# Attention over image pairs: keys and values in PSUM banks of their own, values projected behind the context

## The reference

```python
x0 = _gn(x)                                     # group norm, 32 groups
xn = group_norm(x0, gn1_w, gn1_b, 32)
qkv = einsum('oc,bchw->bohw', qkv_w, xn) + qkv_b   # 3 x 128 rows: 8 heads of 16
q, k, v = split(qkv, 3)                         # q * 0.25
q_norm = softmax(q, axis=-1)                    # over the 256 pixels
k_norm = softmax(k, axis=-2)                    # over the 16 channels of a head
context = einsum('bhdn,bhen->bhde', k_norm, v)
out = einsum('bhde,bhdn->bhen', context, q_norm)
out = einsum('oc,bchw->bohw', out_w, out) + out_b
x = x + group_norm(out, gn2_w, gn2_b, 1) + x0
```

## Time and profile before

| | |
|---|---|
| median of 3 runs | 54.88 us (54.81 to 56.35) |
| the profiled execution | 54.68 us |
| its span, first to last instruction | 52.9 us |
| PE busy | 43.9 us (83%), 434 records |
| PE weight loads busy | 29.2 us (55%) |
| VectorE busy | 41.3 us (78%), 141 instructions |
| ScalarE busy | 30.9 us (58%) |
| GpSimd busy | 26.3 us (50%) |
| mean granted TensorE clock | 0.985 |

### The profile page before, as it was taken

One profiled execution on the slowest core, in us unless ns is written; L12 is line 12 of the kernel. 1 busy time (PEld: TensorE's weight loads), 2 busy tenths in 40 slices (PEclk: granted clock), 3 DMA queues, 4 the chain that ended last, 5 costly groups with the idle time before them and its releaser, 6 DMA issues.

```text
span 52.9 us, 1397 instructions
## 1 busy us (share of the span) xinstructions
PE 43.9 (83%) x434; PEld 29.2 (55%) x434; DVE 41.3 (78%) x141; ACT 30.9 (58%) x98; POOL 26.3 (50%) x55
## 2 busy tenths in 40 slices
PE   2999999993999399569989999998998998995200
PEld 2774747851665346454675666666577464843100
DVE  0039999999998999989699969969969998634730
ACT  0723008949902574599768696696485776358400
POOL 5000221938689218724864984685689920041700
PEclk9999999999999999999999999999999999999985
DMA  0597960000000000000030020021002000020222
GB/s 0 148 323 235 364 221 2 0 0 0 0 0 6 0 0 12 0 0 0 0 105 0 12 97 2 0 74 32 0 1 98 12 0 6 0 93 11 95 99 99
DMA packets 2823, 2.84 MB, mean 54 GB/s; under 512 B 256, under 2 KB 2816, under 8 KB 2816
## 3 DMA queue, kind: packets, MB, share of 16 engines
q1 hardware_dynamic: 2528, 2.49, 14.7%
q10 hardware_dynamic: 288, 0.27, 1.4%
HBM read 1.71 MB, written 1.05 MB: 52 GB/s over the span
## 4 chain that ended last, share of the span: by engine, by line
PE 46%; DVE 31%; issue 13%; ACT 4%; POOL 0%; DVEq 0%; ACTq 0%; POOLq 0%
PE kv_ps L450 8%; PE kv_ps L414 7%; PE o_ps L528 5%; PE o_ps L505 4%; PE q_ps L469 4%; PE kv_ps L438 4%; PE o_ps L491 4%; DVE nqmax L716 3%; PE q_ps L466 3%; DVE kmx L699 3%; DVE ctxm L758 3%; DVE res L800 2%; DVE xstat L599 2%; PE o_ps L516 2%; DVE vs L739 2%
## 5 line engine op out<-in xcount | busy, mean ns | idle before, releaser
L348 ACT ACTIVATE eq<-q_ps,nqmax 128x256 f32<-128x256 f32 x16 | 7.4, 474 | 3.2 <-DVE nqmax L716 3.2
L265 POOL TENSOR_TENSOR orstd<-ve,minus_half 128x1 f32<-128x1 f32 x8 | 4.4, 552 | 9.1 <-DVE ve L782 9.1
L450 PE MATMUL kv_ps<-w_all,xn 64*128 64x256 f32 x64 | 8.3, 379 | 0.0
L414 PE MATMUL kv_ps<-ones 128*128 128x512 f32 x17 | 7.4, 583 | 1.0 <-POOL ones L215 1.0
L246 POOL TENSOR_TENSOR tree<-ek 128x256 f32<-128x256 f32 x7 | 5.1, 725 | 5.3 <-ACT ek L338 5.3
L699 DVE TENSOR_REDUCE kmx<-kv_ps 128x32 f32<-128x512 f32 x8 | 5.5, 684 | 2.1 <-PE kv_ps L450 2.1
L450 PEld LDWEIGHTS kv_ps<-w_all,xn 64*128 64x128 f32 x64 | 6.0, 186 | 0.9 <-issue 0.2
L414 PEld LDWEIGHTS kv_ps<-ones 128*128 128x128 f32 x17 | 4.6, 286 | 2.2 <-POOL ones L215 1.0
L739 DVE TENSOR_TENSOR vs<-kv_ps,rks 128x512 f32<-128x512 f32 x8 | 5.5, 691 | 0.2
L716 DVE TENSOR_REDUCE nqmax<-q_ps 128x2 f32<-128x512 f32 x8 | 5.5, 682 | 0.3 <-issue 0.2
L338 ACT ACTIVATE ek<-ek 128x512 f32<-128x512 f32 x8 | 5.0, 628 | 1.1 <-DVE ek L707 1.1
(11 more groups left out here) (89 smaller groups left out, 87.2 us busy)
## 6 DMA issues: line engine op xcount, KB each, us to landing
out_dram<-res SPq DMA_DIRECT2D x8, 128.0 KB, 1.7
x_sb<-x_dram SPq DMA_DIRECT2D x1, 512.0 KB, 5.4
x_sb<-x_dram SPq DMA_DIRECT2D x2, 128.0 KB, 2.6
x_sb<-x_dram SPq DMA_DIRECT2D x1, 256.0 KB, 4.4
w_all<-weights_dram SPq DMA_DIRECT2D x1, 224.0 KB, 4.5
brow<-b_qkv_dram ACTq DMA_DIRECT2D x1, 192.0 KB, 3.0
mats<-matrices_dram SPq DMA_DIRECT2D x1, 160.0 KB, 5.3
par_avg<-params_dram ACTq DMA_DIRECT2D x1, 67.0 KB, 2.6
```

The source lines that it names most:

```text
L348: last = nc.scalar.activation(eq[:, p % 3, image, :], q_ps[:, image, 0, :], ACT.Exp, bias=nqmax[:, r, image:image + 1], accum_out=qs[:, p ...
L414: nc.tensor.matmul(to, ones[:], ones[:].unsqueeze(1).broadcast_to([P, 4, 128]), start=True, stop=True, skip_group_check=True)
L450: ins = nc.tensor.matmul(kv_ps[r][:, image, chunk, :, :, :], xn[rows(image), r, chunk * 128:(chunk + 1) * 128], w_f[rows(image), KV], star ...
```

## The change

Keys get two banks, `k_ps`, and values two, `v_ps`, one for each image; half of each bank is used. There is thus one set of keys and one of values where there were two of both. `bias` and `keys_values` become `add_bias` and `project`, called once for the keys (`keys(p)`) and once for the values (`values(p)`), each with 128 output columns in a matmul in place of 256 and with its own loads of `xn`. `keys(p)` waits until `key_shift` has read the pair before (`ksub_ready`), `values(p)` until `scale_values` has (`vs_ready`). In a turn `keys(i+1)` stands where `keys_values(i+1)` stood, and `values(i)` comes behind `context(i-1)`. Since the values of a pair now need `xn` a turn later than its keys, `xn` has three buffers. The last pair's context and output go to the first bank of `k_ps`.

```diff
-        xn = sb("xn", [P, 2, PIX])
+        xn = sb("xn", [P, 3, PIX])
...
-        kv_ps = [bank(f"kv_ps{u}", [128, 2, CHUNKS, 2, HEADS, DIM]) for u in range(2)]
+        k_ps = bank("k_ps", [128, 2, 2, CHUNKS, HIDDEN])
+        v_ps = bank("v_ps", [128, 2, 2, CHUNKS, HIDDEN])
...
                 for image in range(2):
-                    wait(act, kv_done[image], p - 1)
-                    wait(act, q_done[image], p - 1)
+                    wait(act, v_done[image], p - 2)
+                    wait(act, q_done[image], p - 2)
...
+            def add_bias(p, to, part):
                 pe.wait_ge(b_ready, 1)
                 for image in range(2):
+                    nc.tensor.matmul(to[:, image, 0, :, :], ones[rows(image), :],
+                                     bsplit[rows(image), part].unsqueeze(1).broadcast_to([CHANNELS, CHUNKS, HIDDEN]),
                                      start=True, stop=False, skip_group_check=True)
...
+            def project(p, to, part, done):
                 for chunk in range(CHUNKS):
                     for image in range(2):
+                        ins = nc.tensor.matmul(to[:, image, 0, chunk, :],
+                                               xn[rows(image), p % 3, chunk * 128:(chunk + 1) * 128],
+                                               w_f[rows(image), part], start=False, stop=(chunk == CHUNKS - 1),
                                                skip_group_check=True)
                         if chunk == CHUNKS - 1:
+                            ins.then_inc(done[image], 1)
+
+            def keys(p):
+                wait(pe, ksub_ready, p)
+                if p > 0:
+                    add_bias(p, k_ps, K)
+                pe.wait_ge(xn_ready[p % 3], p // 3 + 1)
+                project(p, k_ps, K, k_done)
+
+            def values(p):
+                if not there(p):
+                    return
+                wait(pe, vs_ready, p)
+                if p > 0:
+                    add_bias(p, v_ps, V)
+                pe.wait_ge(xn_ready[p % 3], p // 3 + 1)
+                project(p, v_ps, V, v_done)
...
-            keys_values(0)
-            bias(1)
-            keys_values(1)
+            keys(0)
+            values(0)
             queries(0)
+            keys(1)
             warm_up(WARM[3], o_ps[0][:])
...
-            bias(2)
-            keys_values(2)
+            keys(2)
             context(0)
+            values(1)
...
-                bias(i + 1)
-                keys_values(i + 1)
+                keys(i + 1)
                 context(i - 1)
+                values(i)
                 variance(i - 2)
...
             context(PAIRS - 2)
+            values(PAIRS - 1)
             means(PAIRS - 3)
             outputs(PAIRS - 3)
...
                 dve.wait_ge(rks_ready, p + 1)
+                for image in range(2):
+                    dve.wait_ge(v_done[image], p + 1)
```

More of the change, by code:

```diff
@@ L35 @@
 HEAD_MASK = slice(2 * P, 2 * P + TILE)
-Q, KV = slice(0, HIDDEN), slice(HIDDEN, 3 * HIDDEN)
+Q, K, V = (slice(n * HIDDEN, (n + 1) * HIDDEN) for n in range(3))
 FOLDS = CHANNELS + 1
@@ L142, in attention_kernel @@
         coef_ready, rest_ready = sem("coef_ready"), sem("rest_ready")
-        xn_ready = [sem(f"xn_ready{u}") for u in range(2)]
-        kv_done = [sem(f"kv_done{n}") for n in range(2)]
+        xn_ready = [sem(f"xn_ready{u}") for u in range(3)]
+        k_done = [sem(f"k_done{n}") for n in range(2)]
+        v_done = [sem(f"v_done{n}") for n in range(2)]
         q_done = [sem(f"q_done{n}") for n in range(2)]
@@ L327, in affine @@
                 for image in range(2):
[L328 to L331 removed]
+                    wait(act, v_done[image], p - 2)
+                    wait(act, q_done[image], p - 2)
+                nc.scalar.activation(xn[:, p % 3, :], x_sb[:, p, :], ACT.Identity, bias=of(coef_b, p),
+                                     scale=of(coef_a, p)).then_inc(xn_ready[p % 3], 1)
             def key_exp(p):
@@ L441, in bias @@
                                      start=True, stop=False, skip_group_check=True)
-            def keys_values(p):
+            def project(p, to, part, done):
+                for chunk in range(CHUNKS):
+                    for image in range(2):
+                        ins = nc.tensor.matmul(to[:, image, 0, chunk, :],
+                                               xn[rows(image), p % 3, chunk * 128:(chunk + 1) * 128],
+                                               w_f[rows(image), part], start=False, stop=(chunk == CHUNKS - 1),
+                                               skip_group_check=True)
+                        if chunk == CHUNKS - 1:
+                            ins.then_inc(done[image], 1)
@@ L468, in queries @@
                 for image in range(2):
-                    nc.tensor.matmul(q_ps[:, image, 0, :], w_f[rows(image), Q], xn[rows(image), r, :],
+                    nc.tensor.matmul(q_ps[:, image, 0, :], w_f[rows(image), Q], xn[rows(image), p % 3, :],
                                      start=False, stop=True, skip_group_check=True).then_inc(q_done[image], 1)
@@ L544, in variance @@
                                  start=True, stop=True, skip_group_check=True).then_inc(var_done, 1)
-            early = kv_ps[1][:, 0, :, :, :, :]
+            early = q_ps[:, 1, :, :]
             pe.wait_ge(ones_ready, 1)
@@ L551, in _ @@
             warm_up(WARM[1], early)
-            bias(0)
+            add_bias(0, k_ps, K)
+            add_bias(0, v_ps, V)
             group_average(1)
@@ L737, in scale_values @@
                 dve.wait_ge(rks_ready, p + 1)
+                for image in range(2):
+                    dve.wait_ge(v_done[image], p + 1)
                 wait(dve, ctx_done, TILES * (p - 1))
-                nc.vector.tensor_tensor(per_head(vs[:, r, :]), half_of(p, 1), spread(rks[:]),
+                nc.vector.tensor_tensor(per_head(vs[:, r, :]), parts_of(v_ps), spread(rks[:]),
                                         ALU.mult).then_inc(vs_ready, 1)
```

29 lines of the change are left out of this document (12 added, 17 removed).

## The result

The changed kernel takes **55.56 us** (median of 4 runs, 55.36 to 55.71), the kernel before 54.84 (54.58 to 56.35) beside it: ratio 1.0149, 95% interval 1.0118 to 1.0181, so 0.8 us more. The profiled execution took 55.56 us with a span of 53.8 and a mean granted clock of 0.984; before it was 54.68, 52.9 and 0.985.

What follows compares the result with a forecast made beforehand. PE's own stream was taken to bound the kernel, with 0.22 us a turn waiting on ctxm. Start +0.17, loop +0.07, tail +0.86 made +1.1: 55.8 from the profiled 54.68, plus 0.2 for the median: 56.0 us, range 54.7 to 56.9.

Steps and rivals of the forecast that it cites:

- The turn: One round of PE's loop, from one folds to the next: 4.29 us forecast, 0.02 more than before.
- a pair: Two projection matmuls of 128 columns on PE, loads running under the matmul before: 0.113 us, bounds 0.107 and 0.12.
- the wait on `ctxm`: PE's wait for VectorE's masked context ahead of folds: 0.22 us a turn, forecast to go.
- The +0.07 for the loop: Forecast addition to the time from PE's slightly longer turns in the loop: +0.07 us.
- Loads not hidden: Rival: projection loads and columns run in turn, 0.216 us a pair, 60.1 us in all; chance 0.05.
- the loop at VectorE's time: Rival: VectorE's 3.79 us of work sets the loop's turn, giving 54.1 us, or 53.2; chance 0.05.
- PE without seams: Rival: values cost PE only their columns, 0.54 us in place of 0.77, giving 54.8 us; chance 0.12.
- The start: With one key buffer keys(1) waits for key_shift(0); key_max(1) at 11.94 instead of 11.77, whole program 0.17 us later.
- hardly a gap: Claim that VectorE has almost no idle time from key_max(1) to the loop, so the 0.17 us delay passes on.
- The tail: The last pairs: late variance_eps(4), values(7) ahead of outputs(5), then minus_mean(5) and warm-ups delay context(7); +0.86 us.
- the two added semaphores: Extra waits of scale_values for v_done; in the tail vs(7) might follow minus_mean(5) by up to 0.33 us, not 0.11.
- The 0.39 wait of the bias for `vs`: PE's key and value bias load waiting 0.39 us for VectorE's vs before the change; not counted as a cost.

Runs made afterwards that it cites:

- the kernel with the context masked first: The kernel before the change, with mask_context(i-2) ahead of key_max(i) on VectorE, in the loop and behind it: 58.63 us, ratio 1.0698.
- keys moved alone: The changed kernel with only keys(i+1) moved behind queries(i) in PE's loop; VectorE and ScalarE keep their orders: ratio 1.0216.
- gap filled: The changed kernel with PE's, ScalarE's and VectorE's steps reordered, plus seven unread matmuls once between folds(1) and variance(0): ratio 1.0345 to the kernel before.

## Why the prediction was right

The forecast was +1.1 and the profiles show +0.9, by the steps named; as a time it was 56.0, and 55.56 was measured. Of the 0.4 between these two, 0.2 is the 1.1 for 0.9, and 0.2 is the distance of the median before (54.88, of three runs) from the profiled execution (54.68), which the forecast added and which the changed kernel does not have. The errors in the parts all have one sign, and none hid another. The ratio, 1.015, is below the 2% from which the prediction counts a kernel as slower; it gave that outcome 0.51.

- **The turn.** 4.29 forecast, 4.27 to 4.28 measured. Keys and values 0.77 forecast, 0.76 measured; a pair 0.113 forecast, about 0.11 measured; the wait on `ctxm` is gone, and PE itself is late next. The run without the values' bias shows the last point: less work on PE, and the turn is shorter, by 0.11. The +0.07 for the loop was +0.02.
- **Loads not hidden, and the loop at VectorE's time.** Both are ruled out by these rows: pairs 0.11 apart and not 0.216, turns of 4.28 and not 3.79. In this kernel a pair's loads run under the pair before it on the same two row groups. By the rule in "TensorE: Matmul & The Clock Gate" of the Trainium skill, section The mechanism, that loads overlap running matmuls only where the row group differs (the section also names a background weight buffer as a second way), they would not, and here the measurement decides.
- **PE without seams.** The seams are there. The bias in front of the values costs 0.22, of which only 0.11 goes with it; grouping steps of one shape took 0.34 off a turn when PE alone set it. No run separates what of this is the drain at a change of tiling mode ("TensorEngine Tiling (Array Packing)" of the Trainium skill, section Key Properties) and what is the first load, which nothing covers.
- **The start.** `key_max(1)` came at 11.94 to the hundredth, but only 0.11 of the 0.17 reached the loop: VectorE had a little slack between 13.6 and 15.4 (`rks` is 0.16 late there, the next `vs` 0.13, `gvar` 0.09), which "hardly a gap" had counted as none. No run undid this part alone; that it is the one set of banks rests on the 0.78 us wait in the row.
- **The tail.** This is the term that was off: +0.86 forecast, +0.77 measured. The causes and their order were right. `ve(4)` was late by 0.35 and not 0.47 (0.11 of it is the start and loop, which were smaller), and `context(6)` followed `vs(6)` by 0.06 instead of 0.15, so `outputs(5)` was 1.17 late and not 1.39. Two terms were as forecast: `context(7)` starts 1.13 after the warm-ups do, and `nb` to `vs(7)` is 0.20, inside the 0.11 to 0.33. That the two added semaphores make the 0.09 more than before is not shown: with `vs(7)` behind `rks` in both kernels, `rks` to `vs(7)` is 0.47 with them and 0.46 without. The runs on the tail show what the sum alone does not: `minus_mean(5)` ahead of `scale_values(7)` and the warm-ups are each enough to hold `context(7)`.
- **What was dismissed too lightly.** The 0.39 wait of the bias for `vs` was set aside, since `outputs` to a warm-up takes the same 0.56. As a cost it was rightly none. But it marked a ring with 0.2 us of slack, as the kernel with the context masked first showed at 0.5 us a turn.

## What to carry to other kernels

A wait taken out of a full loop is worth only what the engine does not fill with the price of removing it: here 0.22 us of wait went, and 0.22 of work came (keys and values apart take 2 x 0.76, together they took 1.30). The cost showed where nothing covers it, in the last pairs. When two things hold the same instruction, test them alone and together, or each will look free. Before reordering, look for the waits that are almost hidden: here those for `vs` and for `oc`, and the one behind which the clock fell, undid rearrangements that were right in their own sum.

## What the runs showed of the hardware

Each of these kernels has one long wait of PE for the centred values, at 22.8 to 25.5 us. Where it was 0.71 us (the changed kernel), 0.83 (without the values' bias), 0.94 (before), 1.06 (keys moved alone) or 0.17 (gap filled), the granted clock stayed at 1.00, its 2.4 GHz level. In all three in which it was 1.19 us, the clock fell to 0.50, the 1.2 GHz level, within about 1.2 us behind it, for 3 to 4 us. That cost 1.5 us in one turn, more than the wait itself. Seven matmuls that nobody reads prevented it. This is one profile of each kernel; two of the three also waited 0.56 or 0.57 us for `ctxm` just before, and how much waiting is too much is not shown.
